# Gate logits of layers 1 and 2: three thin fp32r products from the split inputs, issued behind the chunk's first up products

## What is computed

```python
# layer 1: input is the state sequence of a GRU over x
gates = (jnp.einsum('bsd,de->bse', x, gate_w) + gate_b) / temperature
weights, indices = jax.lax.top_k(gates, 2)
weights = jax.nn.softmax(weights, axis=-1)
# layer 2: input is gelu of a projection of x
logits = flat @ gate_w + gate_b
weights = jax.nn.softmax(logits, axis=-1)
top_w, top_i = jax.lax.top_k(weights, 2)
```

## Time and profile before

| | |
|---|---|
| median of three runs | 612.05 us (610.6 to 612.27) |
| profiled execution | 611.03 us, of it 609.3 us span from first to last instruction |
| PE busy | 592.0 us, 97% of the span |
| PEld (weight loads) busy | 558.4 us, 92% |
| DVE, ACT, POOL busy | 347.0, 287.2, 113.3 us |
| granted TensorE clock | 0.999 of full, near full in every slice |

### The profile page before, as it was taken

The page is one execution under the profiler, slowest core; times in us unless marked ns, Lnnn a source line. Parts: engine busy times, 40 slices in busy tenths (PEclk is TensorE's granted clock), DMA queues, the critical chain, the costliest instruction groups (busy, mean ns, idle before and its releaser), DMA issues.

```text
span 609.3 us, 12449 instructions
## 1 busy us (share of the span) xinstructions
PE 592.0 (97%) x4510; PEld 558.4 (92%) x4510; DVE 347.0 (57%) x1233; ACT 287.2 (47%) x955; POOL 113.3 (19%) x338
## 2 busy tenths in 40 slices
PE   8899999999999999999999999999999999999996
PEld 8688889889999999999999999999989899898995
DVE  4975766865465454464653555148965673775414
ACT  3365645645655455455564456556833323312210
POOL 4134122111111111111111110000111221312410
PEclk9999999999999999999999999999999999999999
DMA  8999500000000000000000000093202003003000
GB/s 244 319 306 141 60 2 2 2 2 2 1 2 1 2 1 2 2 1 2 2 1 2 1 3 1 1 159 51 105 1 101 9 5 106 4 5 105 10 0 10
DMA packets 47734, 27.06 MB, mean 44 GB/s; under 512 B 28552, under 2 KB 42936, under 8 KB 47160
## 3 DMA queue, kind: packets, MB, share of 16 engines
q1 hardware_dynamic: 45648, 25.77, 19.1%
q10 hardware_dynamic: 2024, 0.48, 0.4%
HBM read 25.68 MB, written 0.57 MB: 43 GB/s over the span
## 4 chain that ended last, share of the span: by engine, by line
PE 85%; DVE 9%; ACT 3%; issue 2%; POOL 0%; DVEq 0%; POOLq 0%
PE Y L1415 35%; PE U L1415 31%; PE ZR L1415 7%; PE HH L1415 7%; PE M L1415 4%; DVE acc_a L849 2%; ACT gated L683 1%; DVE acc_b L849 1%; DVE relu L841 1%; DVE rh L849 0%; DVE cmp_b L841 0%; ACT L696 0%; DVE cmp_a L841 0%; DVE rank L881 0%; ACT scaled_hi L733 0%
## 5 line engine op out<-in xcount | busy, mean ns | idle before, releaser
L1415 PE MATMUL Y<-l_dn,gated 128*128 128x128 f32 x1152 | 162.7, 284 | 1.4 <-DVE acc_a L849 0.7
L1415 PEld LDWEIGHTS Y<-l_dn,gated 128*128 128x128 f32 x1152 | 141.1, 192 | 2.8 <-issue 1.4
L683 ACT ACTIVATE gated<-U,b1T 128x256 f32<-128x256 f32 x256 | 106.9, 474 | 0.0
L1415 PE MATMUL U<-l_x_hi,l_up_hi 128*128 128x256 f32 x256 | 83.0, 324 | 0.0
L665 ACT ACTIVATE h<-ZR,rnn_b 128x8 f32<-128x8 f32 x128 | 34.3, 268 | 86.6 <-PE ZR L1415 84.2
L1415 PE MATMUL U<-l_x_lo,l_up_hi 128*128 128x256 f32 x256 | 72.1, 281 | 0.0
L1415 PE MATMUL U<-l_x_hi,l_up_lo 128*128 128x256 f32 x256 | 71.9, 281 | 0.0
L568 POOL TENSOR_SCALAR zh<-zr_s 128x8 f32<-128x8 f32 x128 | 25.9, 202 | 245.8 <-ACT zr_s L657 245.8
L935 DVE TENSOR_TENSOR_SCAN h_gru<-blend,cand_keep 128x16 f32<-128x16 f32 x128 | 25.0, 195 | 78.0 <-ACT cand_keep L661 76.6
L661 ACT ACTIVATE cand_keep<-HH 128x8 f32<-128x8 f32 x128 | 22.8, 178 | 93.4 <-PE HH L1415 93.4
L1415 PE MATMUL U<-scaled_hi,l_up_hi 128*128 128x256 f32 x192 | 57.5, 300 | 0.0
(11 more groups left out here) (268 smaller groups left out, 1212.2 us busy)
## 6 DMA issues: line engine op xcount, KB each, us to landing
l_bc<-dw SPq DMA_DIRECT2D x4, 1536.0 KB, 6.4
stage<-L_ffn_W_dram SPq DMA_DIRECT2D x4, 768.0 KB, 14.4
w_raw<-L_ffn_W_dram SPq DMA_DIRECT2D x12, 256.0 KB, 7.8
l_up_raw<-L_ffn_W_dram SPq DMA_DIRECT2D x1, 2048.0 KB, 11.4
l_up_raw<-L_ffn_w_dram SPq DMA_DIRECT2D x1, 2048.0 KB, 15.7
l0f_up<-L_ffn_w_dram SPq DMA_DIRECT2D x1, 768.0 KB, 7.8
l0f_dn<-L_ffn_w_dram SPq DMA_DIRECT2D x1, 768.0 KB, 10.2
x<-x_dram SPq DMA_DIRECT2D x1, 512.0 KB, 4.3
```

Of the source, the lines that this page charges most:

```text
L683: last = nc.scalar.activation(gated[:, n % 4, h * N:(h + 1) * N], U[n % 2][:, h * N:(h + 1) * N], ACT.Gelu, bias=b1T[:, col:col + 1])
L1415: return nc.tensor.matmul(out, lhsT, rhs, start=start, stop=stop, skip_group_check=shared)
```

## The change

`gate_w` gets two fp32r parts, made on POOL between the halving of the GRU's weights and the low parts of the up weights. The logits are then `mm3` of the input's parts and the gate weights' parts: three fp32r products of 8 columns for each tile, where there was one f32 product. `logits(n)` is issued behind `project(n)`, in front of the GRU's candidate product. For A it waits for `l1_split` in place of `gru_h`, which `project(n)` has waited for just before. A wait for the gate weights' parts is added at the first place.

```diff
+        gate_parts = [sb("gate_w_" + side, [P, 2, E], F32R) for side in ("hi", "lo")]
...
+        gate_split = sem("gate_split")
...
             pool.wait_ge(gru_scaled, 1)
+            own(nc.gpsimd.tensor_copy(gate_parts[0][:, :, :], gate_w[:, :, :]))
+            nc.gpsimd.tensor_tensor(out=gate_parts[1][:, :, :], in0=gate_w[:, :, :], in1=gate_parts[0][:, :, :],
+                                    op=ALU.subtract).then_inc(gate_split, 1)
...
+                l = int(stream == "B")
+                if (l, k) == (0, 0):
+                    pe.wait_ge(gate_split, 1)
                 if stream == "A":
-                    pe.wait_ge(gru_h, (k + 1) * CT)
-                    m, x = bank("logits0", k), h_states
+                    pe.wait_ge(l1_split, 2 * (k + 1))
                 else:
                     pe.wait_ge(m_free, m_of("zp", k) + 1)
-                    m, x = bank("logits1", k), l2_in
-                for t, xt in enumerate(tiles(x)):
-                    last = mm(m[:, t * E:(t + 1) * E], xt, gate_w[:, int(stream == "B"), :])
+                m = bank(f"logits{l}", k)
+                for t in range(TILES):
+                    last = mm3(m[:, t * E:(t + 1) * E], [x[:, at(t * P, P)] for x in (l1_x, l2_x)[l]],
+                               [w[:, l, :] for w in gate_parts], True, True)
                 last.then_inc(m_full, 1)
...
                     gru_gates_of(step)
+                project(n)
                 logits(n)
-                project(n)
                 for step in gru_steps(n):
```

## The result

| | before | after |
|---|---|---|
| median of 8 runs each | 611.14 us | 613.76 us |
| ratio | | 1.0043, 95% interval 1.0032 to 1.0055 |
| profiled execution, span | 609.3 us | 611.8 us |
| PE busy, records | 592.0 us, 4510 | 592.9 us, 4526 |

The changed kernel is slower by 0.43%, 2.6 us. One run of each eight took about 15 us longer than the rest (in the changed kernel at a mean granted clock of 0.971), as single runs of most kernels here did; these runs are in the medians and not in the ratios. The forecast was 2.94 us, +0.5%, on a median of 612.05; with more runs beside it, the kernel before has 611.14, which explains 0.9 of the 1.2 us between 615.0 and 613.76.

The account below looks back on a forecast made before the run. PE's issue rate was taken as the bound in layers 1 and 2. Terms of 0.70 (A0 to A2), 0.79 (B0 to B2), 0.70 (A3) and 0.75 (B3) summed to 2.94 us, giving 615.0 us, +0.5%, range 612.8 to 616.8.

Parts of the forecast that it names:

- The bound: In layers 1 and 2, PE's issue rate, weight load to weight load, sets the time; added PE work lengthens the run.
- POOL: Two added small gate-weight instructions, estimated at 0.5 us, vanish in POOL's 8.83 us wait for ACT and cost nothing.
- The price of a thin fp32r record: Each 8-column fp32r record in the logits, paced by its weight load, costs PE 0.117 us.
- The upper bound of 0.21: Price per thin record in us if each behaved like the first fp32r matmul behind f32 work, its load not prefetched.
- 47 s - 2.57: Total added time in us over all eight logits blocks, with s the price of a thin record.
- A0 to A2: Layer 1's first three logits blocks: nothing stalls, each pays 0.23 us for its records, 0.70 us together.
- B0 to B2: Layer 2's first three logits blocks: the stall ahead stays, each pays 0.26 us for its records, 0.79 us together.
- A3: Layer 1's last logits block: old logits covered the low-part wait, new ones cannot; the whole block adds 0.70 us.
- B3: Layer 2's last logits block: DVE is the path, idles for later scores and delays PE's weighted sum by 0.75 us.
- Cheap thin products: Rival at all eight blocks: fp32r loads at half the pace, 0.0585 us a record, 0.2 us more, 612.2 us; chance 0.10.
- The stalls swallowed later: Rival: stalls at A3 and B3 are absorbed later, only records cost; 2.0 us more, 614.0 us; chance 0.15.
- Dear thin products: Rival: each thin record costs 0.21 us, 7.3 us more in all, 619.4 us; chance 0.07.

Follow-up runs that it names:

- e1_order_only: Kernel before the change, with only the order changed: its f32 logits issued behind the up products; 612.07 us, ratio 1.0014.
- e9_best_again: As e8_best, but layer 3's score ranking placed between the weighted sum PE waits for and the sum of chunk 2; 608.98 us, ratio 0.9957.
- e11_twelve_f32: Kernel before the change, with its f32 logits issued three times, twelve thin records a place; ratio 1.0129 from three executions.
- e8_best: Kernel before, with layer 2's logits waiting only for the Gelu, a recurrence input product filling A3's wait, and layer 3's ranking one slot later; ratio 0.9984.

## Why the prediction was right, point by point

*The bound.* Right for layers 1 and 2: PE's issue rate. What the eight places cost stands in the time between weight loads, and busy time shows only a third of it. But 0.42 us were lost elsewhere, and the forecast had nothing there (POOL, below).

*The price of a thin fp32r record.* Taken at 0.117, measured 0.113, within the 0.110 to 0.21 of the bounds and near the lower. That each record costs the same is shown by the runs with four, six and twelve of them. That the columns do not set the price follows from 0.113 with 8 columns beside 0.117 with 256; that it is the weight load, and not another cost of every record, is the likely reading and was not tested, since every record here loads 128 columns. The upper bound of 0.21 rested on a misreading: the loads at A0 start evenly, at 126.45, 126.56 and 126.68, and it is the first matmul record that begins early, 0.02 us behind its load, not the second that comes late. With 0.113 in the formula, 47 s - 2.57 is 2.74 us. The two rules of the Trainium skill that I had weighed gave no gain here. The four passes of a true FP32 product (the Trainium skill, FP8 and Floating Point Precision, TensorE Precision Notes) are not its price with 8 columns: four fp32r records cost what the four records of two f32 products do, so three fp32r products cost 1.5 times one f32 product and not three quarters. The fast weight load for types other than FP32 (the Trainium skill, TensorE: Matmul & The Clock Gate, Weight-path perf modes) does not show: the thin fp32r loads last 187 to 192 ns and start 0.11 us apart, the f32 ones 186 to 198 ns.

*A0 to A2, B0 to B2.* Right in mechanism, 0.20 and 0.23 for 0.23 and 0.26, all from the pace.

*A3.* Right in mechanism: the wait was no longer covered, 0.49 us of it stand in the loads. The term was mis-sized by 0.12 us: 0.02 from the pace, 0.09 because the low part of the input came 1.41 us behind the last down loads and not 1.50. The prediction held that fixed. The 0.09 goes back to POOL, which prepares a part (`zh`, then `cand_keep`) of the GRU's update. Before and after, at the last step of the GRU:

```profile
363.78 0.20 POOL L568 TENSOR_SCALAR zh<-zr_s 128x8 f32<-128x8 f32 x1 [2.12 <-ACT zr_s L657]
364.39 0.19 DVE L935 TENSOR_TENSOR_SCAN h_gru<-blend,cand_keep 128x16 f32<-128x16 f32 x1 [0.79 <-POOL cand_keep L569]
...
364.78 0.20 POOL L573 TENSOR_SCALAR zh<-zr_s 128x8 f32<-128x8 f32 x1 [1.83 <-ACT zr_s L662]
365.61 0.19 DVE L940 TENSOR_TENSOR_SCAN h_gru<-blend,cand_keep 128x16 f32<-128x16 f32 x1 [0.70 <-ACT cand_keep L666]
```

POOL starts `zh` 0.46 us behind the end of ACT's `zr_s` before and 0.15 after, so that the update comes 0.56 and 0.48 us behind the last down loads. Such a late start happens once in the 96 GRU steps from A0 to A3 in either kernel, in the changed one at 257.47, where B1's slot shows nothing of it. It stands at A3 in the five profiled kernels without the two new POOL instructions and in none of the eight with them. Why POOL starts late at one step is not shown. DVE's wait for the scores at A3, put at 0.64 us, was 0.43.

But I named the order as the cause at A3, and it is either: the order alone costs 0.46, the products alone 0.58 and both 0.58. Whichever comes first makes the logits wait for the split.

*B3.* Right: 0.70 for 0.75, DVE idle 0.74 for 0.75. The products alone cost nothing there and the order 0.47, which makes it the one place where the order adds to the changed kernel's time, about 0.7 us.

*POOL.* Wrong: the term was put at nothing, and it cost about 0.42 us. The two instructions take 0.19 and 0.22 us, 0.47 from the first to the low parts behind them.

```profile
31.82 0.19 POOL L557 CAST gate_w_hi<-gate_w 128x16 fp32r<-128x16 f32 x1
32.10 0.22 POOL L558 TENSOR_TENSOR gate_w_lo<-gate_w,gate_w_hi 128x16 fp32r<-128x16 f32 x1
32.29 2.68 POOL L564 TENSOR_TENSOR l_up_lo<-l_up_raw,l_up_hi 128x512 fp32r<-128x512 f32 x2
43.80 1.28 POOL L564 TENSOR_TENSOR l_up_lo<-l_up_raw,l_up_hi 128x512 fp32r<-128x512 f32 x1 [8.83 <-ACT l_up_hi L733]
```

The sign that I had named (the idle ahead of the third low part shorter by 0.5, its start unmoved) was not seen: POOL's idle stayed at 8.83 us, and ACT, which releases it, came 0.3 us later. What held ACT up is a DVE instruction that overlaps POOL's first two low parts. Here it is in the kernel before, in the changed one and in `e1_order_only`, with PE's next wait for DVE in the first two:

```profile
33.96 0.84 DVE L841 TENSOR_TENSOR cmp_a<-sig_a 128x128 f32<-128x128 f32 x1 [0.47 <-ACT sig_a L696]
36.64 1.13 PE L1415 MATMUL Y<-l0f_dn,gated 128*128 128x128 f32 x8 [0.38 <-DVE acc_a L849]
...
33.83 1.29 DVE L846 TENSOR_TENSOR cmp_a<-sig_a 128x128 f32<-128x128 f32 x1 [0.47 <-ACT sig_a L701]
36.95 1.13 PE L1420 MATMUL Y<-l0f_dn,gated 128*128 128x128 f32 x8 [0.82 <-DVE acc_a L854]
...
34.61 0.29 DVE L841 TENSOR_TENSOR cmp_a<-sig_a 128x128 f32<-128x128 f32 x1 [0.47 <-ACT sig_a L696]
```

Before, POOL's second low part ended at 34.66 and DVE's instruction at 34.80; in the changed kernel they ended at 34.97 and 35.12; in `e1_order_only` POOL was done at 34.17, ahead of it, and it took 0.29 us. It took 0.84 or 0.85 us in the other three kernels without the two instructions and 1.28 or 1.29 in all eight with them. PE waits 0.44 us longer for DVE behind it, and ACT for PE. From the start of ACT's first conversion of an up weight (26.50 before, 26.36 after) to the start of A0's slot it is 96.48 us before, in `e9_best_again` and in `e11_twelve_f32`, and 96.90 to 96.96 in the changed kernel and the six other kernels with the two instructions whose clock did not fall ahead of A0. No run has the two instructions alone or in another place, but no other edit is common to these kernels ahead of A0.

*The sum.* Near, and in part by luck: the 0.42 us that stood at nothing is made up for by places that cost 0.38 us less than forecast and by the 0.34 us that the stretches between and behind them took less.

*The rivals.* Cheap thin products: fallen. The stalls swallowed later: fallen, 31.05 us behind B3 for 31.08, and the order alone costs 0.46 and 0.47 us. Dear thin products: fallen for six records. One that I did not have: a thin stretch that lowers the clock. Six records a place did not show it; twelve may, and 24 did.

## What to carry to other kernels

Price a product with few columns by its records, each with its weight load, not by its passes or columns: here a split of one f32 product into three fp32r ones goes from two loads to three, and is dearer whatever the type. Before moving a small piece of PE work or giving it another input, look at which waits it covers and who takes its result next, for that was worth as much as the records: at A3 it covered a wait, at B3 it fed an engine that was the path. Work that reads an earlier result than its neighbour does can fill the neighbour's wait (B's logits, 0.18 us a place), and work put off on one engine has to be followed through the queues of the others, since in `e8_best` 1.0 us came back through ACT. Nor is small work free because its engine idles later: POOL had 8.83 us to spare, and 0.47 us ahead of that still cost 0.42.

## What the runs showed of the hardware that I had not expected

The granted clock can fall while PE is 100% busy. After 24 thin records a place (2.7 us in which each streams 8 columns) it was at 1.2 GHz for a good part of what followed at six of the eight places, and the mean clock of the profiled execution was 0.964. The 17.5 us that this cost are as much as the records themselves. After twelve (1.4 us) it fell behind one block of eight in the profiled execution, which may be chance; after six, behind none in the five kernels profiled with six at every place.

A DVE instruction can be held up by POOL: a 128 x 128 TENSOR_TENSOR of 0.29 us took 0.84 and 1.29 us where POOL's TENSOR_TENSOR of 512 columns was running, and ended 0.14 to 0.15 us behind it. The SCALAR_TENSOR_TENSOR just ahead of it (`acc_a<-Y,comb_x,acc_a`), which also ran beside POOL, kept its 0.35 us.
